# Top-k attention with film modulation: the exps and weights of two batches moved into the layer before, a second film buffer, and the shifts' additions moved into the state space stage

## The reference, cut to what matters

```python
Q = (x_text @ Wq).reshape(Bb, Tt, H, DH)
K = (x_vision @ Wk).reshape(Bb, Gg, H, DH)
scores = jnp.einsum('bthd,bghd->bhtg', Q, K) / np.sqrt(DH).astype(np.float32)
...
topv, topi = jax.lax.top_k(scores, K_TOP)
probs = jax.nn.softmax(topv, axis=-1)
...
attn = jnp.zeros_like(scores).at[bi, hi, ti, topi].set(probs)
attn_mean = attn.mean(axis=1)
V = x_vision @ Wv
c_t = jnp.einsum('btg,bgd->btd', attn_mean, V)
c_t = c_t * text_mask[..., None]
x = layernorm(x_text, g_norm_in, b_norm_in)
scale_in, shift_in = jnp.split(c_t @ W_film_in + b_film_in, 2, axis=-1)
x = x * (1.0 + mod_gate * scale_in) + mod_gate * shift_in
y = s4d(x, log_dt, A_re, A_im, C_re, C_im, D_skip)
scale_out, shift_out = jnp.split(c_t @ W_film_out + b_film_out, 2, axis=-1)
y = y * (1.0 + mod_gate * scale_out) + mod_gate * shift_out
xt = x_text + y
h = layernorm(xt, g_ffn, b_ffn)
h = jax.nn.gelu(h @ W1 + b1, approximate=False) @ W2 + b2
xt = xt + h
return layernorm(xt, g_norm_out, b_norm_out)
```

## Time and profile before

| | |
|---|---|
| median of 3 runs | 1179.33 us (1177.02 to 1181.09) |
| profiled execution, its own time | 1170.57 us |
| its span | 1168.8 us |
| mean granted TensorE clock | 0.974 |
| busy: PE, PEld, DVE, ACT, POOL | 91%, 65%, 57%, 48%, 40% of the span |
| `top_attention` in the span | from 365.6 to 416.0 us |

### The profile page before, as it was taken

The page is one execution under the profiler, slowest core; times in us unless marked ns, Lnnn a source line. Parts: engine busy times, 40 slices in busy tenths (PEclk is TensorE's granted clock), DMA queues, the critical chain, the costliest instruction groups (busy, mean ns, idle before and its releaser), DMA issues. The chain is left out here.

```text
span 1168.8 us, 22936 instructions
## 1 busy us (share of the span) xinstructions
PE 1063.2 (91%) x8781; PEld 762.9 (65%) x8781; DVE 671.9 (57%) x2054; ACT 559.2 (48%) x1475; POOL 463.3 (40%) x551
## 2 busy tenths in 40 slices
PE   6999989899997788998998899978899999989996
PEld 5886858577675355676577566645567776666684
DVE  5555553345769847785787467548723126766512
ACT  5434325155676843455445355416543324653432
POOL 7968913122246943883586250012000004041423
PEclk9999989899999699999999999999999999999999
DMA  5000060142205901000000030000011100010312
GB/s 169 1 1 5 2 231 3 68 132 73 79 2 132 288 1 47 1 2 1 1 2 1 1 76 2 2 22 17 15 68 37 36 19 17 1 41 2 131 49 78
DMA packets 55084, 54.18 MB, mean 46 GB/s; under 512 B 19472, under 2 KB 45840, under 8 KB 53952
## 3 DMA queue, kind: packets, MB, share of 16 engines
q1 hardware_dynamic: 54048, 50.84, 14.0%
q0 software_dynamic: 928, 1.88, 0.5%
HBM read 44.08 MB, written 8.63 MB: 45 GB/s over the span
## 5 line engine op out<-in xcount | busy, mean ns | idle before, releaser
L499 POOL TENSOR_TENSOR ln_rstd<-ln_ve,ln_half 128x4 f32<-128x4 f32 x25 | 25.5, 1020 | 250.3 <-DVE ln_ve L457 250.2
L669 DVE TENSOR_REDUCE scratch<-bank 128x4 f32<-128x512 f32 x96 | 63.4, 685 | 31.1 <-PE bank L574 18.1
L1328 ACT ACTIVATE scratch<-bank 128x512 f32<-128x512 f32 x64 | 38.2, 597 | 66.5 <-PE bank L1284 66.4
L730 ACT ACTIVATE scratch<-bank 128x512 f32<-128x512 f32 x96 | 55.5, 598 | 23.4 <-PE bank L589 23.0
L1347 DVE SCALAR_TENSOR_TENSOR x_res<-bank,scratch,x_res 128x128 f32<-128x128 f32 x64 | 18.0, 344 | 82.3 <-PE bank L1294 82.3
L2299 POOL TENSOR_TENSOR scratch<-scratch 128x512 f32<-128x512 f32 x32 | 33.3, 1041 | 79.7 <-DVE scratch L2639 79.7
L1294 PEld LDWEIGHTS bank<-weights,scratch 128*128 128x128 f32 x512 | 59.5, 192 | 7.2 <-issue 7.2
L589 PE MATMUL bank<-ident,scratch 128*128 128x128 f32 x384 | 56.8, 278 | 7.9 <-ACT scratch L724 6.0
L3479 POOL TENSOR_TENSOR scratch<-scratch 128x16 f32<-128x16 f32 x16 | 51.1, 3192 | 29.2 <-DVE scratch L3877 20.7
L1284 PE MATMUL bank<-xnT,weights 128*128 128x512 f32 x128 | 59.4, 608 | 0.7 <-ACT xnT L1317 0.7
L1294 PE MATMUL bank<-weights,scratch 128*128 128x128 f32 x512 | 59.6, 275 | 0.0
(11 more groups left out here) (661 smaller groups left out, 2915.0 us busy)
## 6 DMA issues: line engine op xcount, KB each, us to landing
scratch<-conv_kernels SPq DMA_DIRECT2D x8, 1024.0 KB, 11.3
weights<-e_l_ffn_w SPq DMA_DIRECT2D x20, 256.0 KB, 3.0
scratch<-e_l_ffn_w SPq DMA_DIRECT2D x4, 1024.0 KB, 14.8
values<-scratch SPq DMA_DIRECT2D x8, 512.0 KB, 2.6
scratch<-values SPq DMA_DIRECT2D x8, 512.0 KB, 4.4
weights<-w_l_ffn SPq DMA_DIRECT2D x1, 3698.0 KB, 16.2
scratch<-e_l_ffn_w SPq DMA_DIRECT2D x4, 768.0 KB, 7.0
weights<-w_l_attn SPq DMA_DIRECT2D x1, 2560.5 KB, 9.3
```

The costliest lines, as they stand in the source:

```text
L669: self.nc.vector.tensor_reduce(self.top[:, n % 4, :], self.by_head(self.core.ps[n % 4][:, :]), AX_X, ALU.max, negate=True).then_inc(self.t ...
L730: self.nc.scalar.activation(self.prob_of(n), self.by_head(self.core.ps[4 + n % 2][:, :]), ACT.Exp, scale=scale) \
L1328: nc.scalar.activation(hT[u % 2][:, i, :], ps[UP_BANKS[i]][:, :], act_func) \
```

## The change

- In the causal attention: the small root instructions of the inputs' first half (`begin_roots`) go from turn 15 to turn 14 on POOL. ACT takes `e` of batch 0 at the start and `e_left` of batch 0 at the end of turn 14, and both of batch 1 in turn 16 (where batch 0's were). POOL does the whole difference, weight and product of batch 0 in turn 15, and the difference of batch 1 in turn 16.
- In `top_attention`: POOL's loop begins with batch 1's weight and runs one turn earlier than before; the inputs' second half goes from t = 3 to t = 2. `film_in` has two buffers. The additions of the normed rows to `shift_out` leave POOL's loop. PE transposes batch 0's mean right behind the values, and has two filler products at the end in place of four. ACT takes the film parts of batch b in the same turn as its mean and text, and the exps of all keys two batches ahead; the last batch's `e_left` comes behind mean and text of batch 6. The Gelu table load leaves the block.
- In `state_space_out`: POOL adds the normed rows to `shift_out` in two halves of four batches before the first group, and the bias additions to x come before groups 1 and 3. ACT loads the Gelu table behind the eight copies.
- Buffers are placed elsewhere in scratch and in the weights' buffer; no DMA is added, removed or moved.

```diff
 # layer_l1_attn, POOL
+                if n == STEPS - 2:
+                    pool.wait_ge(ahead.rstd.sem, ahead.half(ahead.rstd, 0))
+                    begin_roots(core, link, search, 0)
                 if n == STEPS - 1:
...
-                    begin_inputs(core, link, pool, search, inputs_at, g_in, b_in, 0)
+                    begin_inputs(core, link, search, inputs_at, g_in, b_in, 0)
+                    pool.wait_ge(best_left.sem, best_left.at(0))
+                    link(nc.gpsimd.tensor_tensor(search.e_left0, search.e0, search.e_left0, ALU.subtract))
+                    search.pool_weight(link, 0)
+                    link(nc.gpsimd.tensor_tensor(search.e_left0, search.e_left0,
+                                                 search.weight.unsqueeze(2).broadcast_to([P, 4, P]), ALU.mult))
+                if n == STEPS:
+                    pool.wait_ge(best_left.sem, best_left.at(1))
+                    link(nc.gpsimd.tensor_tensor(search.e_left1, search.e1, search.e_left1, ALU.subtract))
 # layer_l1_attn, ACT (best_exps and best_exps_left hold the four activations each that stood in turn 16)
                 if n == STEPS:
                     next_keys()
+                    best_exps(1, search.e1)
+                    best_exps_left(1, search.e_left1)
+                if n == STEPS - 2:
+                    best_exps(0, search.e0)
                 u = finished(n)
...
                 if n in AHEAD_LAST:
                     empty_ahead(*AHEAD_LAST[n])
+                if n == STEPS - 2:
+                    best_exps_left(0, search.e_left0)
 # top_attention
-    film_in = spare.take(2, P)
+    film_in = c.take(4, P)
 # top_attention, POOL
+            norm.pool(pool, 1)
             for t in range(1, B + 2):
-                if t == 3:
+                if t == 2:
...
-                if t - 1 < LAST:
-                    left_out = e_left[(t - 1) % 2]
+                if t < LAST:
+                    left_out = e_left[t % 2]
...
-                if 0 <= t - 3 < LAST:
-                    b = t - 3
+                if 0 <= t - 2 < LAST:
+                    b = t - 2
...
-                    pool.wait_ge(film_out.sem, film_out.at(4 * b + 3))
-                    nc.gpsimd.tensor_tensor(shift_out[:, b, :], shift_out[:, b, :], core.xn[:, b, :], ALU.add)
 # top_attention, PE
+            mean(0)
             norm.pe(pe, 1, TURN_BANK)
...
-            for t in range(2, B + 2):
-                b = t - 2
+            for b in range(B):
                 open_film(b)
+                if b > 0:
+                    mean(b)
+                if b > 0 and b + 4 < B:
+                    score(b + 4)
...
-            core.keep_clock_bf(SCORE_BANKS[3], 4)
+            core.keep_clock_bf(SCORE_BANKS[3], 2)
 # top_attention, ACT
-                if b > 0:
-                    act.wait_ge(modulated.sem, modulated.at(b - 1))
+                if b > 1:
+                    act.wait_ge(modulated.sem, modulated.at(b - 2))
...
-            for t in range(2, B + 3):
-                if FIRST <= t <= B:
-                    exps_left(t - 1)
-                if t - 2 < B:
-                    take_mean(t - 2)
-                if t < B:
-                    exps(t)
-                if t + 3 < B:
-                    copy_scores(t + 3)
-                if 0 <= t - 2 < B:
-                    take_text(t - 2)
-                if 0 <= t - 3 < B:
-                    take_film(t - 3)
-                if t == B:
-                    core.load_table(ACT.Gelu)
+            for b in range(1, B):
+                if FIRST <= b + 1 < LAST:
+                    exps_left(b + 1)
+                take_mean(b)
+                if b + 4 < B:
+                    copy_scores(b + 4)
+                if b == 1:
+                    take_film(0)
+                take_text(b)
+                if b + 1 == LAST:
+                    exps_left(LAST)
+                if FIRST < b + 2 < B:
+                    exps(b + 2)
+                take_film(b)
 # state_space_out, ACT
+            core.load_table(ACT.Gelu)
 # state_space_out, POOL
+            for h in range(2):
+                if h == 1:
+                    pool.wait_ge(film_taken.sem, film_taken.at(1))
+                link(nc.gpsimd.tensor_tensor(shift_out[:, in_half(h), :], shift_out[:, in_half(h), :], core.xn[:, in_half(h), :],
+                                             ALU.add))
             for g in range(GROUPS - 1):
+                if g in (1, 3):
+                    h = g // 2
+                    nc.gpsimd.tensor_tensor(core.x[:, in_half(h), :], core.x[:, in_half(h), :], every(b_out), ALU.add) \
+                        .then_inc(x_biased.sem, x_biased.up())
```

More of the change, by code:

```diff
@@ L2115, in begin_inputs @@
     link(tt(rstd, var, core.ln_half[:, rows], ALU.pow))
+def begin_inputs(core, link, search, u, g_in, b_in, h):
+    rows = slice(B // 2 * h, B // 2 * (h + 1))
+    rstd, part = search.rstd[:, rows], u[:, rows, :]
+    every = lambda a: a.unsqueeze(1).broadcast_to([P, B // 2, D])
+    tt = core.nc.gpsimd.tensor_tensor
     link(tt(part, core.xn[:, rows, :], rstd.unsqueeze(2).broadcast_to([P, B // 2, D]), ALU.mult))
@@ L2135, in __init__, with pool_weight @@
         kept = Carve(core.scratch)
-        kept.at = SCRATCH - (SLOTS + 1) * H * P
-        assert c.at <= kept.at
-        self.e_left0, self.left = kept.take(H, P), kept.take(SLOTS * H, P)
+        kept.at = self.start = SCRATCH - (SLOTS + 3) * H * P
+        self.e1, self.e_left1, self.e_left0, self.left = (kept.take(n * H, P) for n in (1, 1, 1, SLOTS))
         self.tops, self.removed, self.negated = (core.count(n) for n in ("values_made", "removed", "negated"))
+    def pool_weight(self, link, b):
+        nc, weight = self.nc, self.weight
+        link(nc.gpsimd.tensor_tensor(weight, self.tot[:, b % 2, :], self.tot_left[:, b % 2, :], ALU.subtract))
+        link(nc.gpsimd.tensor_tensor(weight, weight, self.minus_one, ALU.pow))
+        link(nc.gpsimd.tensor_scalar(weight, weight, self.core.text_on[:, b:b + 1], 1.0 / self.H, ALU.mult, ALU.mult))
     def heads(self, b):
@@ L2188, in layer_l1_attn @@
     prob, probT = c.take(2 * 8, P).rearrange("p (r s) k -> p r s k", r=2), c.take(2, BANK)
-    top, total, inv = (c.take(2, 8) for _ in range(3))
     oT = c.take(2 * H, P).rearrange("p (r h) t -> p r h t", r=2)
     yT, y = c.take(2, P), c.take(2, D)
-    rest = c.take(4 * P)
     following = Carve(core.beside_next.tensor)
@@ L2198, in layer_l1_attn @@
     keys_next, queries_next = following.take(B * P), following.take(B * P)
-    search = BestKeys(core, c, following, 0)
+    search = BestKeys(core, following, 0)
+    top, total, inv = (following.take(2, 8) for _ in range(3))
+    assert c.at <= search.start
+    rest = search.e1.rearrange("p h k -> p (h k)")
     by_own_head = w.take(2 * 4, P).rearrange("p (b h) k -> p b h k", b=2)
@@ L2511, in next_keys, with best_exps, best_exps_left @@
                 nc.scalar.copy(keys_next[:, half(1)], ps[S_BANKS[1]][:, :]).then_inc(keys_out.sem, keys_out.up())
+            def best_exps(b, e):
+                act.wait_ge(search.negated.sem, search.negated.at(b))
+                for h in range(4):
+                    a = nc.scalar.activation(e[:, h, :], search.s[:, 4 * b + h, :], ACT.Exp, bias=search.nmax[:, b, h:h + 1],
+                                             accum_out=search.tot[:, b, h:h + 1])
+                a.then_inc(best_exped.sem, best_exped.up())
+            def best_exps_left(b, e_left):
+                act.wait_ge(search.removed.sem, search.removed.at(search.round_at(b, 3, 1)))
+                for h in range(4):
+                    a = nc.scalar.activation(e_left[:, h, :], search.left[:, 4 * b + h, :], ACT.Exp,
+                                             bias=search.nmax[:, b, h:h + 1], accum_out=search.tot_left[:, b, h:h + 1])
+                a.then_inc(best_left.sem, best_left.up())
             def empty_ahead(kind, b=0):
@@ L4145, in top_attention @@
     slot = lambda b, h: b % SLOTS * H + h
-    e, e_left = [search.e0, c.take(H, P)], [search.e_left0, c.take(H, P)]
-    tot, tot_left, weight = search.tot, search.tot_left, c.take(H)
+    e, e_left = [search.e0, search.e1], [search.e_left0, search.e_left1]
+    tot, tot_left, weight = search.tot, search.tot_left, search.weight
     meanT, ctT = c.take(P), c.take(P)
-    film_in = spare.take(2, P)
-    minus_one, last_weight = c.take(H), c.take(H)
+    film_in = c.take(4, P)
+    last_weight = c.take(H)
+    assert c.at <= search.start
     half = lambda h: slice(h * BANK, h * BANK + BANK)
@@ L4250, in _, with mean @@
                     m.then_inc(values_made.sem, values_made.up())
+            def mean(b):
+                if b == 0:
+                    pe.wait_ge(values_out.sem, values_out.at(0))
+                elif b < LAST:
+                    pe.wait_ge(kept.sem, kept.at(b - 1))
+                else:
+                    pe.wait_ge(last_kept.sem, last_kept.at(0))
+                if b > 0:
```

(6 more changed lines are left out.)

106 lines of the change are left out of this document (41 added, 65 removed).

## The result

| | before | after |
|---|---|---|
| median of 17 runs each, same chip | 1179.42 us (1177.02 to 1181.37) | 1183.05 us (1180.75 to 1188.07) |
| profiled execution, its own time | 1170.57 us | 1183.05 us |
| its span, mean granted clock | 1168.8 us, 0.974 | 1181.3 us, 0.966 |

The change makes the kernel slower: the ratio is 1.0038, 95% interval 1.0029 to 1.0046. The forecast was +1.6 us; the medians differ by 3.6 us and the ratio stands for 4.5.

What follows compares the result with a forecast made beforehand. DVE's search fills most of `top_attention`; POOL and ACT hold its end. `e_left` of batch 6 at 401.9 plus 15.7 gives 417.6 against 415.98, +1.6 us; state space 0. On the median: 1179.33 + 1.6 = 1180.9 us, range 1174.8 to 1185.0.

Steps and rivals of the forecast that it cites:

- my own case: Whole kernel: +1.6 us, own range -0.5 to +3.5, chance 0.50.
- the rival in which PE stays at 1.2 GHz to the end and into the convolution: Top attention's tail and convolution: +3.8 us and up to 1.8 more, 1183.1 to 1184.9 us; chance 0.18.
- Block start: End of the causal attention: POOL's last addition comes later, so the block ends 0.2 us later (bounds 0 and 0.5).
- Turns: ACT in `top_attention`: 6.34 us a turn at 1.2 GHz, 5.32 at 2.4; taken as two at 6.34, one at 5.8.
- First such turn: ACT in `top_attention`: the turn with batch 0's film parts and batch 1's text ends at 383.4 us (381.9 to 384.3).
- From there to the end: `top_attention`, from `e_left` of batch 6 to the block's end: 15.7 us against 14.62 before; 15.0 to 16.5 by clock.
- State space: `state_space_out`: POOL's additions, the Gelu table and fewer fillers cost 0; a low clock there at most 1.8 us.
- POOL's relief: `top_attention`: without the 0.45 us addition per batch, POOL's turn falls from 5.24 to some 4.8 us and waits for ACT.
- The second film buffer: Tail of `top_attention`: saves the 0.36 us that ACT waited for POOL before film parts.
- Nothing moves: Rival: lost and won ends cancel, the top attention ends within 0.8 us of 415.98, time 1179.3; chance 0.18.
- the search becomes the bound: Rival in `top_attention`: the last `e_left` starts when DVE's search ends, at 404.5; -4.0 us, 1175.3; chance 0.14.
- the port pair: Tail of `top_attention`: DVE and POOL share SBUF ports; POOL holding up DVE would make +2.0 of +1.6; nothing added.

Runs made afterwards that it cites:

- e7: Changed kernel, but POOL takes batch 1's difference at the start of the top attention instead of in the causal attention; ratio 1.0029 to the kernel before.
- e9: e5 with batch 1's difference at the start of the top attention and batch 6's film parts ahead of the mean of batch 7; ratio 0.9984.
- e1: Changed kernel, but the last batch's `e_left` stands ahead of the mean of batch 6; ratio 1.0033 to the kernel before.
- e8: Changed kernel, but the additions of the normed rows to the shifts stand in POOL's top attention loop again, only batch 7's later; ratio 1.0033.
- e10: e5 with one film buffer in place of two; ratio 0.9994 to the kernel before.
- e3: Changed kernel with film parts one turn later, the last `e_left` ahead of the mean of batch 6, and exps ahead of the text copy; ratio 0.9995.
- e5: e3 with the last `e_left` again behind mean and text of batch 6, as in the changed kernel; ratio 0.9972 to the kernel before.
- e12: Changed kernel with only the film parts taken one turn later; ratio 1.0007 to the kernel before.
- e6: e5 with PE fillers in the last two turns: three ahead of each mean, one ahead of each text product, six at the end; ratio 0.9983.
- e4: Changed kernel with four filler products on PE ahead of each text product; ratio 1.0038 to the kernel before.

## Why the forecast was right, and where it was too small

The direction and the mechanism held: ACT, no longer POOL, holds the turns, the film product is exposed in them, and the kernel is slower by 0.38%. The likeliest time was 2 to 3 us too low, so the outcome lies just above my own case (to +3.5) and close to the rival in which PE stays at 1.2 GHz to the end and into the convolution, which I had given 0.18 and which asked for 3.8 us and up to 1.8 more.

- **Block start.** Forecast +0.2 (bounds 0 and 0.5), measured +0.36. The row of POOL shows it: the last addition follows batch 1's difference without a gap. What I had not seen is that undoing it wins nothing further on (e7, e9), since DVE's normalisations then get longer by as much.
- **Turns.** Forecast 6.34 us at 1.2 GHz and 5.32 at 2.4 GHz; measured 6.32 (four times, in the changed kernel and e7) and 5.27. The order of the steps within a turn was read rightly. The sum of the three was 18.5 and came to 17.60.
- **First such turn.** `e_left` of batch 3 was to start at 383.4; in the frame of the kernel before it started at 381.68 + 3.26 = 384.94 in the changed kernel, and at 383.51 in e1. So the estimate fits e1 and is 1.5 too early for the changed kernel. Of the difference 1.25 us is already there at `e_left` of batch 2 (20.79 and 19.54), behind the value products at the block's start (2.91 us and 2.02). That the turns then came 0.9 shorter than summed is luck: the third ran mostly at 2.4 GHz. So `e_left` of batch 6 came at 402.54 for my 401.9, +0.64, and at 402.45 in e1, which started in time and had no turn under 6.30.
- **From there to the end**: the term that was mis-sized. Forecast 15.7, with 15.0 and 16.5 as bounds; measured 16.83, above the upper one. Against the sum at 2.4 GHz the mean, the text and half a film product took 0.34, 0.30 and 0.66 us more (411.19 to 412.28, 412.28 to 413.42, 413.42 to 415.00), which is 1.3 us of the 1.5 that I had as the price of the low clock and of which I took 0.7. The rest is mainly 0.48 us between `e_left` and the mean copy of batch 6, 6.89 for 6.41: text of batch 5 waited (the 1.44 in ACT's row) for a mean and fillers at half clock.
- **State space.** Forecast 0, measured +0.66, all of it the low clock at the convolution's start (2.41 us for the first 64 products) and a later start behind fillers at 1.2 GHz. I had its bound of 1.8 in the rival and left it out of the sum. That the additions and the table load cost nothing there is shown by e7 and e8.
- **POOL's relief**: the shifts' additions out of its loop are worth nothing in this order (e8), as forecast. **The second film buffer**: forecast 0.36; with one buffer ACT waits 0.35 us in e10's row, and the block ends 0.26 us later from the last `e_left` on.
- **Nothing moves**, and **the search becomes the bound**: the first did not come; the second did, but only with the film parts one turn late (e3: `e_left` 7 at 53.02, search until 53.45), and e5 then ended the block 3.2 us earlier than the kernel before (61.67 for 64.83; forecast 4.0), of which 2.0 are left at the up product.

Of the port pair I had added nothing. POOL's modulation at 409.86 started while DVE's L4431 ran (409.65 to 410.33) and took 0.79 us for 0.46; DVE's L4432 started at 410.36, while that modulation ran until 410.65, and took 0.83 us against 0.69 for the same instruction in the earlier trace rows. e5 has the same 0.83. The Trainium skill ("SBUF — State Buffer", section on the two separate sides) lets either engine be the one that waits. The trace agrees in direction, with 0.33 us for POOL and 0.14 for DVE; held until POOL's end, DVE's instruction would have taken 0.98.

What stays open: in single executions the clock phase moves this stretch by 2 us, so the last half microsecond of any two ways is not evidence, and the 0.5 us by which the changed kernel's times lose more than its way is not explained (for e7 the two agree: 3.4 us by its ratio, 3.25 by its way). The medians of e5 and e9, whose traces agree within 0.05 us, have ratios 0.9972 and 0.9984; both intervals lie below 1. The version to keep is e5: faster than the kernel before by 0.2 to 0.3%, and 0.6% faster than the changed one (0.9972 / 1.0029, e7 being run beside it).

## What to carry to other kernels

When work is moved to relieve one engine, write down the new order of the next engine and look in it for a copy that stands in the same turn as the product it reads: one turn of delay there was worth 4.5 to 4.7 us of the way here (e12 against e7 and e8), more than the whole loss. How much depends on the clock of the engine that it waits for, so price the turn at both levels. A place in a queue is good or bad only together with its neighbours' timing: the last `e_left` behind the text copy won 1.6 us of the block once ACT was early, and lost 1.1 to 1.9 while it was late. And price a tail of short dependent steps on PE at the low clock, the first products of the next block included, as soon as the trace of before shows one stretch of it there.

## What the runs showed of the hardware

- The granted clock is not a property of the kernel. The same instructions, in e5 and e6, had 0.84 and 0.59 from 375 to 395 us, PE's film product of batch 1 took 1.13 us in one and 2.07 in the other, and `e_left` of batch 6 differed by 2.1 us.
- A busier PE had the lower clock: 15.19 of 20 us at 0.50 in e7, 13.68 of 20 at 0.84 in e5. The busy time is in part the effect of the clock (a film product takes 2.07 us for 1.13), so it can't be read as its cause. The Trainium skill ("TensorE: Matmul & The Clock Gate", Part 1) lets activity release the higher level. With fillers the clock was higher, 0.87 in e4 where the same order had 0.57 to 0.71 and 1.00 from 405 to 415 us in e6 where e5 had 0.65 and 0.66. But they stand in the same queue as the products that matter: two of them took 1.06 us at 1.2 GHz.
- A normalisation on DVE (128x128) took 0.70 us beside POOL's difference in e7 and 0.69 in e9, and 0.33 to 0.37 in e5 and e8, where POOL had only small instructions there.
